# Gated products of the shared expert written to SBUF instead of PSUM, in a four-layer conditional residual kernel

## What is computed

```python
def _gemma_mlp(x, gate_w, up_w, down_w):
    g = jnp.einsum('bsh,hi->bsi', x, gate_w)
    u = jnp.einsum('bsh,hi->bsi', x, up_w)
    return jnp.einsum('bsi,ih->bsh', jax.nn.gelu(g, approximate=True) * u, down_w)
...
out = out + _gemma_mlp(x, shared_gate, shared_up, shared_down)
...
x = x + _L0_cond_ref(x, cond_8, ...)
x = x + _L1_cond_ref(x, cond_8, ...)
x = x + _L2_cond_ref(x, cond_8, ...)   # top-2 routed experts + the shared expert
x = x + _L3_cond_ref(x, cond_8, ...)   # one expert per row, silu(gate) gating
```

## Time and profile before

| | before |
|---|---|
| median of 3 runs | 139.98 us |
| lowest and highest | 138.63, 140.18 us |
| profiled execution | 138.68 us |
| its span | 136.9 us |
| busy: PE, DVE, ACT, POOL | 132.6, 102.2, 99.3, 75.3 us |

### The profile page before, as it was taken

How to read it: one execution, slowest core, us unless ns; L and a number is a source line. 1 busy time by engine, 2 the same in 40 slices (tenths; PEclk the granted TensorE clock), 3 DMA queues, 4 the chain that set the end, 5 groups by cost and what they waited for, 6 DMA issues and landing times.

```text
span 136.9 us, 3163 instructions
## 1 busy us (share of the span) xinstructions
PE 132.6 (97%) x866; PEld 121.0 (88%) x866; DVE 102.2 (75%) x201; ACT 99.3 (73%) x205; POOL 75.3 (55%) x89
## 2 busy tenths in 40 slices
PE   6999999999999999999999999999999999999991
PEld 5978887878888899999999999999999999999990
DVE  0699898797766677578886787867868677887792
ACT  3774797969964669777797777756757669889870
POOL 0238369776991046477486774863542635325770
PEclk9999999999999999999999999999999999999999
DMA  4999999997001976564774656746577476565134
GB/s 139 343 403 408 409 400 397 403 400 304 4 0 74 385 304 266 229 255 187 306 290 180 268 217 279 287 186 268 208 286 296 171 306 242 210 249 226 41 115 153
DMA packets 11345, 34.54 MB, mean 252 GB/s; under 512 B 1088, under 2 KB 2368, under 8 KB 11328
## 3 DMA queue, kind: packets, MB, share of 16 engines
q1 hardware_dynamic: 11184, 34.21, 63.8%
q10 hardware_dynamic: 144, 0.13, 0.3%
HBM read 12.32 MB, written 1.05 MB: 98 GB/s over the span
## 4 chain that ended last, share of the span: by engine, by line
PE 97%; DVE 0%; issue 0%
PE up L293 34%; PE gate L293 32%; PE acc L293 31%; DVE x_res L997 0%; DVE slabs L827 0%; DVE shift_pick L828 0%
## 5 line engine op out<-in xcount | busy, mean ns | idle before, releaser
L766 POOL TENSOR_TENSOR dn_lo<-slabs,dn_hi 128x256 fp32r<-128x256 f32 x40 | 29.7, 742 | 41.0 <-ACT dn_hi L649 41.0
L625 ACT ACTIVATE h_act<-gate 128x512 f32<-128x512 f32 x48 | 28.8, 599 | 26.6 <-PE gate L293 25.2
L917 DVE TENSOR_TENSOR h_pair<-up,h_pair 128x512 fp32r<-128x512 f32 x55 | 37.5, 682 | 0.0
L927 DVE SCALAR_TENSOR_TENSOR up<-h_act,w_route,up 128x512 f32<-128x512 f32 x32 | 24.2, 755 | 16.9 <-PE up L293 16.9
L293 PE MATMUL gate<-x_hi,w_gu 128*128 128x256 f32 x160 | 35.3, 281 | 0.0
L293 PE MATMUL up<-x_hi,w_gu 128*128 128x256 f32 x158 | 34.9, 282 | 0.0
L631 ACT ACTIVATE h_pair<-up 128x512 fp32r<-128x512 f32 x55 | 32.8, 596 | 0.0
L293 PEld LDWEIGHTS gate<-x_hi,w_gu 128*128 128x128 f32 x160 | 27.5, 188 | 0.2
L293 PE MATMUL acc<-h_pair,dn_hi 128*128 128x512 f32 (+1 forms) x76 | 27.6, 378 | 0.0
L293 PEld LDWEIGHTS up<-x_hi,w_gu 128*128 128x128 f32 x158 | 27.1, 188 | 0.0
L293 PE MATMUL gate<-x_lo,w_gu 128*128 128x256 f32 x80 | 22.5, 282 | 0.0
(11 more groups left out here) (127 smaller groups left out, 204.1 us busy)
## 6 DMA issues: line engine op xcount, KB each, us to landing
w_gu<-slabs SPq DMA_DIRECT2D x40, 512.0 KB, 3.0
slabs<-slabs_moe SPq DMA_DIRECT2D x8, 768.0 KB, 13.1
slabs<-slabs_l SPq DMA_DIRECT2D x4, 768.0 KB, 8.4
outT<-x_res SPq DMA_DIRECT2D x7, 128.0 KB, 2.0
sh_raw<-slabs_shared SPq DMA_DIRECT2D x2, 384.0 KB, 5.2
x_res<-x_rest SPq DMA_DIRECT2D x1, 768.0 KB, 7.0
slabs<-second_in SPq DMA_DIRECT2D x1, 320.0 KB, 3.1
slabs<-third_in SPq DMA_DIRECT2D x1, 256.0 KB, 3.8
```

What stands on the lines that cost most here:

```text
L625: nc.scalar.activation(h_act[:, u % 2, :], gate_ps[u % 2][:], ACT.Gelu_apprx_tanh).then_inc(act_done, 1)
L766: nc.gpsimd.tensor_tensor(dn_lo[:, q % W_SLOTS, :], slab_cols(at, DOWN_AT, 256), dn_hi[:, q % W_SLOTS, :].bitcast(F32), ALU.subtract).then ...
L917: V.tensor_tensor(h_lo[:, u % H_SLOTS, :], h_of(u), h_hi[:, u % H_SLOTS, :].bitcast(F32), ALU.subtract).then_inc(h_lo_done, 1)
L927: ins = V.scalar_tensor_tensor(h_of(u), h_act[:, k, :], weight, h_of(u), ALU.mult, ALU.mult)
```

## The change

The products of the 16 shared units are written to SBUF. `h_of(u)`, which names where product(u) is put and where round_h(u) and lo_h(u) read it, gives for a shared unit a slot of 512 columns in `sh_raw`; three slots are used in turn (0 to 511, 512 to 1023, 1024 to 1535). product(u) reads the up bank explicitly. Before the slots are written for the first time, product(0) and product(1) wait until POOL has read the first and both halves of `sh_raw`. From the fourth unit on, product(u) waits until lo_h(u-3), the last reader of its slot, is done. The routed units and L3 keep their products in the PSUM banks. The number and the order of the instructions on every engine stay as they were, and PE's waits are unchanged.

```diff
         def h_of(u):
 
+            if u < UNITS_SHARED:
+                return sh_raw[:, (u % 3) * 512:(u % 3 + 1) * 512]
             return up_ps[u % 4][:] if u < T0 else l3_up[(u - T0) % 3][:]
...
                 dve.wait_ge(act_done, u + 1)
                 dve.wait_ge(up_ready, u + 1)
                 if weight is None:
-                    ins = V.tensor_tensor(h_of(u), h_act[:, k, :], h_of(u), ALU.mult)
+                    if u < 2:
+                        dve.wait_ge(sh_lo_ready, u + 1)
+                    elif u > 2:
+                        dve.wait_ge(h_lo_done, u - 2)
+                    ins = V.tensor_tensor(h_of(u), h_act[:, k, :], up_ps[u % 4][:], ALU.mult)
```

## The result

| | before | after |
|---|---|---|
| median of 6 runs each | 139.49 us | 143.16 us |
| lowest and highest | 138.63, 140.18 | 142.52, 143.59 |
| profiled execution | 138.68 us | 143.23 us |
| its span | 136.9 us | 141.4 us |

The ratio is 1.0286, 95% interval 1.0248 to 1.0323: the change costs about 4.0 us (3.5 to 4.5). The forecast was 143.4 us, a loss of 4.1 us on a base of 139.3 us.

The account below looks back on a forecast made before the run. PE, ending the chain for 97% of the 136.9 us span, bounds the kernel. Five lateness terms summing to 4.1 us gave 142.8 on the profiled execution and 144.1 on the median; the middle, 143.4, was taken, 8-in-10 range 141.0 to 147.2.

Parts of the forecast that it names:

- the walk: Step-by-step timing of lo_h and POOL collisions through the shared stage to the first w_gu load, summing to 4.1 us.
- its five terms: PE's added lateness: 1.45 at shared_down(5), 0.45, 0.85, 0.85 by lo_h(9) to (11), 0.55 at the w_gu load.
- lo_h stands until POOL's instruction is done: Shared stage: lo_h with two SBUF inputs waits out POOL's SBUF-reading subtraction, up to 2.41 us per collision.
- nothing is held: Rival: lo_h beside L759 is not held, nothing leaves its slack, time 138.7 to 140.0 us; chance 0.08.
- both go slower: Rival: lo_h and POOL share the reader, lo_h at most doubles its streaming to 1.2 us, 140.4 us; chance 0.06.
- POOL is held by lo_h, by up to 0.53: Expert subtractions: a streaming lo_h holds POOL; bounds 0 and 0.53 us, of which 0.53 was taken.
- The rival without it (141.0 us): Rival: only DVE waits, POOL is not held by lo_h; PE ends 2.3 to 2.5 us late; chance 0.12.
- A waiting lo_h gets in between back-to-back POOL instructions: Expert subtractions: lo_h and POOL alternate, 2.95 us a round against PE's 2.10.
- the rivals in which lo_h starves (145.5 and more): Rival: waiting lo_h is not let in between back-to-back POOL instructions; 6.8 us late, 145.5 to 146.8; chance 0.10.
- shared_down(5) 1.45 late: Shared stage: lo_h(5), held by a POOL expert subtraction, is done at 31.95, while PE wanted it at 30.55.
- e4: POOL's expert-weight subtraction (L759), at 32.16 before: about 2.6 later, then held by lo_h(7), running 35.0 to 37.4.
- The weights, +0.55: First routed matmul: POOL's last expert subtraction ends at 46.2, w_gu lands at 50.1, PE would be there at 49.55.

Follow-up runs that it names:

- memsets: Changed kernel with POOL's eight expert subtractions each replaced by two memsets: ratio 1.0; kernel before with the same memsets: 0.9996.
- unit 2 alone: The change applied to shared unit 2 only, the other 15 shared units keeping product, round_h and lo_h on PSUM: ratio to before 1.0017.
- the halves: Changed kernel with POOL's eight 128x1024 subtractions each cut into two of 128x512: 1.0312, +4.3 us; kernel before with the same cut: 1.0041, +0.6 us.
- lo_h's operand alone: Kernel before with only lo_h of the shared units reading sh_raw slots in SBUF: ratio 1.024, +3.3 us, median 143.15 us.
- the run with a gap of 4.7 us on PE: Kernel before with two more POOL subtractions of 128x1024 ahead of the last one: ratio 1.0441, +6.1 us.

## Why the prediction was right

The loss (4.0 us, 3.5 to 4.5, for 4.1), its places and their order came out as the walk had them; the rows that carried it, and the earlier trace rows, are small instructions elsewhere in the kernel. That the sum comes so close is partly luck: against the measured lateness its five terms are off by +0.29, -0.16, -0.15, -0.14 and +0.08 us, which nearly cancel. The base of 139.3 us was a choice too; the six runs of before have their median at 139.49.

- **The waits cost nothing, the durations nothing.** Shown: everything but lo_h's operand gives 0.9999. product 672 ns and round_h 632 ns lie within the bounds taken.
- **lo_h stands until POOL's instruction is done.** Shown: lo_h(2), (5) and (8) to (11), six as forecast, end 0.55 us after a subtraction. Reading SBUF is the condition on POOL's side: none is held beside memsets. The rivals by which nothing is held, or both go slower, fall.
- **POOL is held by lo_h, by up to 0.53.** This had no row. It was right, the size a little less: 0.45 for each of three in e4 to e7. The rival without it (141.0 us) falls.
- **A waiting lo_h gets in between back-to-back POOL instructions.** Also without a row, also right: one lo_h between every two of e4 to e7, and PE lost 0.7 a round there, where 0.85 was forecast, since a round is 2.38 + 0.45 = 2.83 us and not 2.95. That rules out the rivals in which lo_h starves (145.5 and more).
- **shared_down(5) 1.45 late.** Measured 1.74. Of the 0.29, 0.10 is that PE starts 0.15 us after the lo_h it waits for (32.56 to 32.71), where the walk had 0.05. The other 0.19 is a later lo_h(5), and a collision that the walk left out accounts for it: lo_h(1) holds POOL's w_rest for 0.31 us, so e0 starts 20.11 - 0.42 = 19.69 instead of 19.38 and lo_h(2), with all behind it, comes later. With unit 2 alone, where lo_h(1) reads PSUM, e0 and lo_h(2) are on the walk's times.
- **A wait of PE that the walk did not see.** PE had been late already, 0.75 at shared_down(4). The x2 matmuls behind unit 5 wait for `keep_x2(2)` (token pair 2's write of x_res, L907; the row at 24.90), and shared_down(4) for `keep_x2(3)`; both stand behind the held lo_h(2) on DVE. The walk followed the delay of 1.11 through DVE and ACT, but looked on PE's side only for who waits for lo_h. The run with unit 2 alone shows this wait by itself (0.31); most of the rest of the 0.75 comes with the later e0. It did not spoil the sum because shared_down(5) would have waited for lo_h(5) anyway; the later of two waits counts.
- **e4.** The walk had it start at 35.0, held by lo_h(7). It started at 35.45 - 0.42 = 35.03, but it took its usual 2.42 us and had waited for ACT's rounding (3.44, the row above): the right time for another reason.
- **The weights, +0.55.** Measured 4.07 - 3.44 = 0.63. The path was right, and two sizes were off against each other. The slack is 0.15 us and not 0.39: the prediction took 2.9 us for the load, the shortest of all, where this one takes 3.0, and left out the 0.14 from its landing to PE's start. And e7 ended at 46.32 - 0.42 = 45.90, earlier than the 46.2 of the walk.
- **The clock.** Rightly small here. The gaps were short (0.8 us at most); in these runs the clock fell after the gaps of 3.0 and 4.7 us and not after 0.8 and 2.2.

One expectation behind the prediction was wrong, that of the halves: it named that more lo_h would hold POOL, but put the whole loss at 1 to 2.5 us, where POOL alone gave away 5.0 in eleven holds. What stays open: whether the two places in memory play a part (every pair that excluded each other lay in different tiles, but none was moved), and how much of the first part of the walk depends on which of lo_h and POOL comes first by chance. In the two traces with the whole collision (after, lo_h's operand alone) the order was the same.

## What to carry to other kernels

Before an operand is moved from PSUM to SBUF, count the SBUF inputs of every VectorE instruction that reads it: with two of them it and GpSimd's instructions that read SBUF took turns here. lo_h stood until the 2.4 us instruction was done, and GpSimd stood for about half a microsecond in return, though before the change VectorE was busy for only 75% of the span and GpSimd for 55%. Follow a stall through the engine's queue to everything behind it (here the token splits and, over ScalarE, the expert weights), since the instruction that stalls was late for its own consumer in only four of six cases. And where the engine that bounds the kernel (here PE) waits for nothing in the profile of before, a change of the other engines' operands has nothing to win, so the question is only what it can break.

## What was not expected of the hardware

That GpSimd is held by VectorE too, and that the two alternate even if GpSimd's instructions stand back to back (10.87 us for four instead of 9.52), was assumed in the forecast without a row; it is now measured. What was not expected is that shorter GpSimd instructions don't lessen the total: in halves GpSimd lost 5.0 us to VectorE instead of 1.8, and the kernel stayed 4.3 us slower than before. And in the run with a gap of 4.7 us on PE the time was some 1.3 us longer than PE's lateness of 4.8 us behind the gap, with the granted clock at 0.50 for about three microseconds.
